# A masked graph aggregation on one core: x loaded from two queues, layernorm's scale moved behind the matmuls, differences in batches of four

## The reference, cut to what matters

```python
h = jnp.maximum(_layernorm(x, axis=-1), 0.0)        # x: 4096 x 64
support = h @ weight                                # 64 x 64
mask = (adj != 0)                                   # adj: 4096 x 4096, ones at random, 1 in 256
rank = jnp.cumsum(mask, axis=1)
deg = rank[:, -1:]
k = jnp.minimum(deg, 100.0)
pos = rank - (deg - k)
w = mask * jnp.where(pos > 0, 0.5 ** (k - pos), 0.0)
out = x + w @ support + bias
```

## Time and profile before

| | us |
|---|---|
| median of 3 runs | 232.07 (232.03 to 232.62) |
| the profiled execution | 232.5 |
| its span, first to last instruction | 230.1 |
| PE busy | 201.8 (88% of the span) |
| DVE busy | 197.7 (86%) |
| ACT busy | 163.7 (71%) |
| POOL busy | 26.0 (11%) |

### The profile page before, as it was taken

The page is one execution under the profiler, slowest core; times in us unless marked ns, Lnnn a source line. Parts: engine busy times, 40 slices in busy tenths (PEclk is TensorE's granted clock), DMA queues, the critical chain, the costliest instruction groups (busy, mean ns, idle before and its releaser), DMA issues.

```text
span 230.1 us, 6364 instructions
## 1 busy us (share of the span) xinstructions
PE 201.8 (88%) x2768; PEld 196.3 (85%) x2768; DVE 197.7 (86%) x227; ACT 163.7 (71%) x303; POOL 26.0 (11%) x53
## 2 busy tenths in 40 slices
PE   0005898899999999999999999999999899899994
PEld 0004885899999999999999999999999789899993
DVE  1799999997799989999979999969999999677053
ACT  2203489767877988878887878887889798787610
POOL 8921000411000010110010001000000000000000
PEclk9999999999999999999999999999999999999999
DMA  5999999999999999999999999999700000000001
GB/s 182 227 214 194 215 216 216 216 216 216 212 215 216 215 214 211 215 219 216 215 215 219 218 214 220 212 218 218 158 20 3 11 3 14 0 14 3 11 14 29
DMA packets 8074, 36.11 MB, mean 157 GB/s; under 512 B 1648, under 2 KB 3440, under 8 KB 3952
## 3 DMA queue, kind: packets, MB, share of 16 engines
q0 software_dynamic: 4608, 33.56, 70.1%
q1 hardware_dynamic: 3136, 2.10, 3.5%
q10 hardware_dynamic: 304, 0.07, 0.1%
HBM read 68.22 MB, written 1.05 MB: 301 GB/s over the span
## 4 chain that ended last, share of the span: by engine, by line
PE 71%; DVE 17%; issue 4%; DMA 4%; ACT 3%; POOL 1%; POOLq 0%
PE acc L570 31%; PE chain L563 22%; PE chain L561 13%; DVE masks L310 6%; DMA adj_b<-in_adj 4%; DVE part L316 3%; DVE powers L369 2%; PE acc L524 2%; ACT support L255 2%; DVE powers L362 2%; PE chain L549 1%; PE acc L514 1%; ACT powers L266 1%; DVE later L353 1%; DVE sums L344 1%
## 5 line engine op out<-in xcount | busy, mean ns | idle before, releaser
L266 ACT ACTIVATE powers<-chain 128x512 int16<-128x512 f32 (+1 forms) x282 | 152.3, 568 | 39.3 <-PE chain L563 31.3
L570 PE MATMUL acc<-support,powers 128*128 128x192 bf16 x1024 | 167.5, 246 | 2.8 <-issue 1.3
L563 PE MATMUL chain<-diag_own,masks 128*128 128x128 bf16 x640 | 125.6, 231 | 0.0
L561 PE MATMUL chain<-diag_past,masks 128*128 128x128 bf16 x596 | 118.5, 224 | 3.0 <-ACT powers L266 2.9
L570 PEld LDWEIGHTS acc<-support,powers 128*128 128x128 bf16 x1024 | 101.1, 102 | 4.5 <-DVE powers L369 1.7
L563 PEld LDWEIGHTS chain<-diag_own,masks 128*128 128x128 fp8e3 x640 | 91.0, 147 | 0.0
L561 PEld LDWEIGHTS chain<-diag_past,masks 128*128 128x128 fp8e3 x596 | 84.8, 145 | 5.0 <-ACT powers L266 4.7
L310 DVE TENSOR_SCALAR masks<-adj_b 128x4096 uint8<-128x4096 bf16 x32 | 72.9, 2279 | 3.8 <-DMA adj_b<-in_adj 3.8
L563 PE MATMUL chain<-diag_step,masks 128*128 128x128 bf16 x384 | 62.2, 220 | 0.0
L563 PEld LDWEIGHTS chain<-diag_step,masks 128*128 128x128 fp8e3 x384 | 52.1, 145 | 0.0
L206 POOL DMA_DIRECT2D adj_b<-in_adj x32 | 18.7, 585 | 116.3 <-DVE masks L310 111.8
(11 more groups left out here) (45 smaller groups left out, 53.0 us busy)
## 6 DMA issues: line engine op xcount, KB each, us to landing
adj_b<-in_adj POOLq DMA_DIRECT2D x32, 1024.0 KB, 30.3
x_sb<-in_x SPq DMA_DIRECT2D x2, 512.0 KB, 4.7
out<-x_sb SPq DMA_DIRECT2D x14, 64.0 KB, 2.6
out<-x_sb SPq DMA_DIRECT2D x4, 32.0 KB, 9.3
w<-in_L_gnn_weight ACTq DMA_DIRECT2D x2, 16.0 KB, 4.6
bias_b<-in_L_gnn_bias ACTq DMA_DIRECT2D x1, 32.0 KB, 4.5
```

Source lines behind the costliest of these rows:

```text
L266: nc.scalar.activation(powers[:, c, b, cols].bitcast(i16), chain[c][:, cols], ACT.Relu, bias=(MAX_NEIGH + 1) * STEP).then_inc(powers_ready ...
L561: nc.tensor.matmul(chain[c][:, at:at + P], column(n, t + 1), diag_past[:, :], start=False, stop=False, skip_group_check=True)
L563: return nc.tensor.matmul(chain[c][:, at:at + P], column(n, t), diag_own[:, :] if marked else diag_step[:, :], start=False, stop=True, ski ...
L570: return nc.tensor.matmul(acc[u % ACCS][:, k * 3 * D:(k + 1) * 3 * D], powers[:, u % FLIGHT, s + 1 if k < MARKS[u] else s, at:at + P], sup ...
```

## The change

- x's second half is issued by ACT's queue, ahead of the weights and the bias, instead of by SP behind the first. A half now consists of the upper or lower four rows of each eight, so that each partition's half is four pieces of 1 KB (before: two of 2 KB).
- POOL issues the first four loads of adj ahead of the six `affine_select` that build the constants. It no longer centers half 1; DVE does.
- The squares, the centered rows and the transposed rows live in the buffer `powers`; `adj_b` has 8 slots and the ring of masks 12. Unit 1's and unit 2's first `weigh` waits until these are free.
- `normalize` is gone. PE transposes the centered rows (relu commutes with a positive scale) before slot 0, and DVE multiplies the product with the weights by the reciprocal deviation where it lies, in PSUM (`scale`, four of 128 x 512). The transposes and the four products with the weights stand ahead of slot 0 (the fourth in slot 1), the parts in slots 0 to 7. The four blocks have a bank each, those of `acc`.
- Products of unit 0 start in slot 7 (before: 14); units 1 and 2 start in slots 5 and 6 (before: 5 and 10), unit 3 in slot 14 (before: 15).
- BATCH is 4. MARKS go from 2, 1, 2, 1, 1, ... to 2, 2, 0, 2, 2, 0, ... for units of two: 19 loads are marked instead of 20. Scans and halvings of a unit stand one slot earlier.
- On DVE's opening, `mask(1)` stands ahead of `scan(0, 0)`. The bias is added in four pieces, in slots 14, 17, 48 and 71.
- A way to let ACT make masks is added (`signs`), but the set of loads that would use it, `SIGNED`, is empty.

```diff
-    BATCH = 8
-    LOADS = 7
-    RING = 10
+    BATCH = 4
+    LOADS = 8
+    RING = 12
-    MARKS = [1, 1, 1, 2, 1, 2, 1, 1, 2, 1, 1, 2, 1, 1, 0, 0, 1, 1]
-    STARTS = [0, 5, 10, 15, 22, 28, 33, 39, 45, 50, 56, 62, 67, 73, 79, 84, 90, 96]
-    LAGS = [14, 10, 8, 11, 11, 11, 11, 11, 11, 11, 11, 11, 11, 11, 11, 11, 11, 8]
+    MARKS = [1, 1, 1, 2, 2, 0, 2, 2, 0, 2, 2, 0, 2, 2, 0, 0, 0, 0]
+    STARTS = [0, 5, 6, 14, 23, 27, 34, 40, 46, 51, 57, 63, 68, 74, 80, 85, 91, 97]
+    LAGS = [7, 5, 8, 11, 11, 10, 11, 10, 10, 11, 11, 12, 12, 12, 11, 11, 10, 9]
+    SIGNED = {}
...
-            return tensor[:, :, :].rearrange("p (h e t) d -> p e h t d", h=2, e=2)[:, 1 - f]
+            return tensor[:, :, :].rearrange("p (r e t) d -> p e r t d", r=RUNS, e=2)[:, 1 - f]
...
         def _(sp):
-            for f in range(2):
-                sp.dma_start(half_of(x_sb, f), half_of(x.rearrange("(p t) d -> p t d", t=T), f))\
-                  .then_inc(x_loaded[f], 16)
+            sp.dma_start(half_of(x_sb, 0), half_of(x.rearrange("(p t) d -> p t d", t=T), 0)).then_inc(x_loaded[0], 16)
...
+            for n in range(4):
+                load(n)
             pool.wait_ge(zeroed, 6)
...
-            for n in range(4):
-                load(n)
...
-            pool.wait_ge(mean_ready, 2)
-            nc.gpsimd.tensor_tensor(half_of(cen, 1), half_of(x_sb, 1), spread(mean, 1),
-                                    ALU.subtract).then_inc(cen_ready[1], 1)
...
         def _(act):
+            act.dma_start(half_of(x_sb, 1), half_of(x.rearrange("(p t) d -> p t d", t=T), 1)).then_inc(x_loaded[1], 16)
             act.wait_ge(w2_zeroed, 2)
...
+                if g == 0:
+                    part(1, 0)
+                if g == 1:
+                    part(0, 0)
+                if g == 2:
+                    part(2, 0)
+                    part(3, 0)
+                if g == 3:
+                    part(0, 1)
+                    part(1, 1)
+                if g == 4:
+                    part(2, 1)
+                    part(3, 1)
+                if g == 5:
+                    part(0, 2)
+                    part(2, 2)
+                if g == 6:
+                    part(3, 2)
+                if g == 7:
+                    part(1, 2)
...
+            def scale(i):
+
                 dve.wait_ge(ln_step, 6)
-                dve.wait_ge(cen_ready[f], 1)
-                nc.vector.tensor_tensor(half_of(cen, f), half_of(cen, f), spread(rstd, f),
-                                        ALU.mult).then_inc(unit_rows, 1)
+                dve.wait_ge(support_ready, i + 1)
+                of_block = rstd[:, :].rearrange("p (r i two) -> p r i two", i=4, two=2)[:, :, 3 - i, :]
+                block_of = split[i][:, :].rearrange("p (r two d) -> p r two d", two=2, d=D)
+                nc.vector.tensor_tensor(block_of, block_of, of_block.unsqueeze(3).to_broadcast([P, RUNS, 2, D]),
+                                        ALU.mult).then_inc(scaled[i], 1)
...
             row_sums(0)
+            means(0)
             row_sums(1)
-            means(0)
+            center(0)
             means(1)
-            center(0)
-            square_sums(0)
+            center(1)
+            sq_sums(0)
             mask(0)
+            sq_sums(1)
             halve_1(0)
-            square_sums(1)
+            variance()
+            halve_3(0)
             halve_2(0)
-            halve_3(0)
+            mask(1)
             scan(0, 0)
-            variance()
-            mask(1)
             halve_1(1)
             deviation()
             halve_2(1)
+            scale(1)
             halve_3(1)
+            scale(0)
             scan(1, 0)
-            normalize(0)
+            scale(2)
+            scale(3)
             mask(2)
...
             pe.wait_ge(consts_ready, 6)
+            turn_h(0)
+            turn_h(1)
+            make_support(0)
+            turn_h(2)
+            make_support(1)
+            turn_h(3)
+            make_support(2)
             for g in range(SLOTS):
```

More of the change, by code:

```diff
@@ L104, in gnn_decay_kernel @@
         x_sb = sb("x_sb", [P, T, D], fp32)
-        cen = sb("cen", [P, T, D], fp32)
-        h_t = sb("h_t", [P, T // 2, P], fp32)
-        sq = adj_b[:, LOADS - 1, :].bitcast(fp32).rearrange("p (t d) -> p t d", d=D)
+        own_room = powers[:, 2, :, :].rearrange("p s c -> p (s c)")
+        cen = own_room[:, 0:2 * T * D].bitcast(fp32).rearrange("p (t d) -> p t d", d=D)
+        h_t = own_room[:, 2 * T * D:4 * T * D].bitcast(fp32).rearrange("p (a b) -> p a b", b=P)
+        sq = powers[:, 1, :, :].rearrange("p s c -> p (s c)")[:, 0:2 * T * D].bitcast(fp32)\
+            .rearrange("p (t d) -> p t d", d=D)
         row_sum, mean, sq_sum, var_eps, std, rough, newton_a, newton_b, newton_c, rstd = (
@@ L122, in gnn_decay_kernel @@
         acc = [pb(f"acc{a}", [P, 512], fp32) for a in range(ACCS)]
-        turned = (acc[0], acc[1])
-        split = (acc[2], acc[3])
+        spare = pb("spare", [P, 512], fp32)
+        turned = (spare, chain[2])
+        split = acc
         x_loaded = [sem(f"x_loaded{f}") for f in range(2)]
@@ L140, in gnn_decay_kernel @@
         std_ready = sem("std_ready")
-        unit_rows = sem("unit_rows")
         h_turned = sem("h_turned")
         h_t_ready = sem("h_t_ready")
[L144 to L147, removed]
+        support_ready = sem("support_ready")
+        scaled = [sem(f"scaled{i}") for i in range(4)]
+        part_taken = [sem(f"part_taken{i}") for i in range(4)]
+        part_ready = [sem(f"part_ready{i}") for i in range(4)]
         xb_ready = sem("xb_ready")
+        signs_ready = sem("signs_ready")
         mask_ready = sem("mask_ready")
@@ L246, in turn_h, with part, signs @@
                 act.wait_ge(h_turned, i + 1)
-                t = 4 * BLOCKS[i]
-                nc.scalar.activation(h_t[:, t:t + 4, :], turned[i % 2][:, :].rearrange("p (a b) -> p a b", a=4),
+                nc.scalar.activation(h_t[:, 4 * i:4 * i + 4, :], turned[i % 2][:, :].rearrange("p (a b) -> p a b", a=4),
                                      ACT.Relu).then_inc(h_t_ready, 1)
[L251 to L256, removed]
+            def part(i, s):
+                if s:
+                    act.wait_ge(part_taken[i], s)
+                else:
+                    act.wait_ge(scaled[i], 1)
+                nc.scalar.activation(steps_of(support[:, :, s, :], i),
+                                     split[i][:, :].rearrange("p (r two d) -> p r two d", two=2, d=D),
+                                     ACT.Copy).then_inc(part_ready[i], 1)
+            def signs(n, j):
+                act.wait_ge(adj_loaded[n % LOADS], 16 * (n // LOADS + 1))
+                if n >= RING:
+                    u = UNIT_OF[n - RING]
+                    act.wait_ge(chain_ready[u % FLIGHT], taken_until(u) + TAKEN[u])
+                at = slice(j * N // PIECES, (j + 1) * N // PIECES)
+                nc.scalar.activation(masks[:, (n + SHIFT) % RING, at].bitcast(i8), adj_b[:, n % LOADS, at],
+                                     ACT.Sign).then_inc(signs_ready, 1)
             def weigh(u, b):
@@ L264, in weigh @@
                 act.wait_ge(chain_ready[c], taken_until(u) + b + 1 - (MARKS[u] == SIZES[u]))
+                if u in (1, 2) and b <= 1:
+                    if u == 1:
+                        act.wait_ge(sq_sum_ready, 2)
+                    else:
+                        act.wait_ge(support_ready, 4)
                 cols = slice(0, SIZES[u] * CHAINS[u] * P) if b else plain(u)
@@ L300, in _ @@
                             weigh(u, g - STARTS[u])
+                for n in SIGNED:
+                    if 0 <= g - SIGNED[n] < PIECES:
+                        signs(n, g - SIGNED[n])
+                if g == 0:
[18 more added lines that the diff above has]
+                    part(1, 2)
         @block.vector
@@ L305, in mask @@
             def mask(n):
+                if n in SIGNED:
+                    dve.wait_ge(signs_ready, PIECES * (1 + sum(m < n for m in SIGNED)))
+                    two = masks[:, (n + SHIFT) % RING, :].bitcast(u16)
+                    nc.vector.tensor_scalar(two, two, 0x0101, None, ALU.bitwise_and).then_inc(mask_ready, 1)
+                    return
                 dve.wait_ge(adj_loaded[n % LOADS], 16 * (n // LOADS + 1))
@@ L475, in _ @@
                         floor(u, (g - STARTS[u] - 1) // BATCH - 1)
+                if g == 14:
+                    add_bias(0)
+                if g == 17:
+                    add_bias(1)
+                if g == 48:
+                    add_bias(2)
+                if g == 71:
+                    add_bias(3)
                 for u in range(NU):
@@ L482, in _ @@
                         mask(FIRST[u] + 1)
+                    if u >= 3 and to == 7:
+                        halve_1(u)
                     if u >= 3 and to == 6:
-                        halve_1(u)
-                    if u >= 3 and to == 5:
                         halve_2(u)
@@ L490, in _ @@
```

(22 more changed lines are left out.)

103 lines of the change are left out of this document (27 added, 76 removed).

## The result

| | before | after |
|---|---|---|
| median of 4 runs, us | 232.34 (232.03 to 232.64) | 224.09 (223.27 to 224.81) |
| profiled execution | 232.5 | 224.8 |
| its span | 230.1 | 222.5 |
| PE, DVE, ACT busy | 201.8, 197.7, 163.7 | 202.5, 203.0, 161.7 |

The ratio is 0.964 (95% interval 0.960 to 0.968): 8.3 us faster, where 5.8 were forecast. (With a fourth run the kernel before has its median at 232.34, 0.3 above the one that the forecast started from.) The time lies in the range given and in the forecast's own.

The account below looks back on a forecast made before the run. PE was taken as the bound, DVE second: unit 3's base 42.6, matmuls 173.2, stalls 5.2, tail 3.3 and 2.4 outside the span make 226.7, less 0.4: 226.3 us. Range 223.5 to 235; the forecast's own 223.5 to 229.5.

Parts of the forecast that it names:

- unit 3's base: Landmark ending the opening, from which PE hardly rests: forecast at 42.6 us, against 43.02 before.
- matmuls left, at 0.082 and 0.060: PE's work after the landmark: 988 products at 0.082 us, 1536 counts and bases at 0.060, together 173.2 us.
- stalls and last drain: PE's waits after the landmark plus the final drain: 5.2 us, against 5.8 before; bounds 3 and 8.
- tail to the span's end: From PE's last product to the end of the profiled span: 3.3 us, as before.
- outside the span: Time of the profiled execution not covered by its span: 2.4 us.
- median below it: The profiled execution lay 0.4 us above the median, so 0.4 is taken off.
- ACT's pace to slot 9: In the opening, ACT's powers and parts set the pace for 12.5 us, until 36.5.
- rival 1: DVE keeps all its idle time and reaches mask 31 only at 183 us: 229.5 us in all; chance 0.16.
- rival 2: In the opening, x takes turns with adj's loads and lands after 14 us, not 6.6: 235 us; chance 0.20.

Follow-up runs that it names:

- after_again: The changed kernel run once more, unaltered (also called the repeat): 224.26 us, ratio 0.965.
- scan_first: Changed kernel with scan(0, 0) put ahead of mask(1) again: 223.72 us, ratio 0.963.
- adj_after_consts: Changed kernel with adj's first four loads issued behind the six constants again: 224.57 us, ratio 0.967.
- opening_alone: Changed kernel's opening and starts with the MARKS of before, BATCH 8 and lags of 11 from unit 3 to 16: 233.74 us, ratio 1.006.
- tables alone: Kernel before with only BATCH 4 and the changed kernel's MARKS, its own starts, lags and opening: 227.31 us, ratio 0.979.
- x_one_queue: Changed kernel with x's second half issued on SP's queue behind the first half: 240.35 us, ratio 1.033.
- x_one_adj_late: Changed kernel with both halves of x on SP's queue and adj's first loads behind the constants: 224.78 us, ratio 0.968.
- both_fillers: Changed kernel with scan(0, 0) ahead of mask(1) and 44 filler matmuls behind the fourth product with the weights: 223.31 us, ratio 0.961.
- pe_kept_busy: Changed kernel with 44 filler matmuls into an idle PSUM bank where PE idles before slot 2: 223.55 us, ratio 0.962.
- no_bias: Changed kernel without the four bias additions and their waits, so the output lacks the bias: 223.74 us, ratio 0.962.
- batch_8: Changed kernel with differences over eight steps (BATCH 8 for 4), its marks, starts and lags kept: 247.11 us, ratio 1.059.

## Why the prediction was right, and where it was off

| term | predicted | measured |
|---|---|---|
| unit 3's base | 42.6 | 42.02 (40.99 in the repeat) |
| matmuls left, at 0.082 and 0.060 | 173.2 | 173.2 |
| stalls and last drain | 5.2 | 219.23 - 42.02 - 173.2 = 4.0 |
| tail to the span's end | 3.3 | 3.3 |
| outside the span | 2.4 | 2.3 |
| profiled execution | 226.7 | 224.8 |
| median below it | 0.4 | 0.7 |

**The landmark** was near, though one step in it was wrong. It came 0.6 us early in the first profile and 1.6 in the second, where the low clock lasted half as long, so on the second it is the larger miss; I had 41.5 for a clock that stays up. adj's first load was to land 1.7 us earlier. It was issued 1.8 us earlier and mask(0) still started at 11.90, where it was 11.8 before: adj's packets came behind x's. The cost was small, since DVE was not at mask(0) before 11.15 in any case. Unit 0's base (20.45 for 19.9), its first power (23.6 for 23.4) and `scale` (0.689 for 0.65) came as worked out, and so did ACT's pace to slot 9 (37.1 for 36.5). That PE had to wait 2.1 us for the weights was not foreseen; it cost nothing that scan_first or adj_after_consts could find.

**The matmuls** were a count from the program, and the numbers left at unit 3's base are those of the trace, 988 and 1536. (The 36 products done by then are 28 of unit 0 and eight of unit 1, not 32 and four.) Moving products into light slots is worth its 2.6 us only because PE is the bound after them.

**The stalls** were mis-sized too, by 1.2 us. I took 2.0 us off for differences that are ready earlier. From the starts in the trace, less matmuls at the two prices, PE's stalls from slot 80 on were 2.9 us before and none after; from slot 14 to 40 they rose from 2.6 to 4.1, where I had 0.8 and 0.6 more. The third row of before that I had read, DVE's differences holding PE's weight loads for 1.7 us, showed only part of the late stalls: the rest stood there as "issue".

**DVE** did run behind PE and was no bound. Its last mask came at 181.17, inside the 176 to 183 worked out, its busy time rose by 5.3 us (6.6 predicted), the differences took 31.6 us for 26. Taking 2.7 us off it gained nothing that can be told from zero. What rival 1 feared, a start made earlier that DVE gives back, does happen without the slack: opening_alone, the same opening with the tables of before, loses 1.5 us. The three numbers don't add: tables alone 5.0 us faster, opening alone 1.5 us slower, both 8.3 us faster. Of the 8.3, some 4.7 are there only with both. My sum had them as terms side by side, and a reader who took the opening's terms alone from it would have forecast a gain. The sum came out because all its terms were changed at once.

**x** was there at 6.0, so rival 2 did not come true, but its mechanism is real and the margin small: the second half issued 0.7 us later, in its first half's queue, turns 224 into 240. I had priced it at 235 and put its edge at a landing of 12.4 us. x_one_queue landed at 25.3 and lost 16.3 us, so a microsecond of landing cost 0.84 us. The Trainium skill says that a DMA engine goes round its queues packet by packet (DMA: Bandwidth & Descriptors, "Queues, rings and completion order"). The stragglers of x_one_queue agree with it; the pieces of x that were ahead of adj did not take turns with anything, and the second half's first pieces came only behind the first half's, although in another queue. The same page ("Issuing engines are not separate DMA queues") says that issuing from several engines saves only the sequencer's time. For x's speed that holds (x_one_adj_late is as fast). But beside adj's early loads the second queue, with its issue 0.69 us earlier, was worth 16 us, and I had put it at nothing. Whether those 0.69 us did it, as the page would have it, or the queue as such, no run shows.

**What the falls of the clock cost.** In the profiles, a low clock for 3.4 us costs nothing at unit 3's base: it comes at 40.9 to 41.0 in after_again, scan_first and both_fillers, and at 40.9 to 41.3 in the four variants without a fall. Longer falls go with a later base, 42.02 in the changed kernel (6.8 us) and 41.60 in adj_after_consts (10.2 us). Of the eight runs of the changed kernel the two with a clock of 1.0 throughout took 223.3 and 223.8 us, the one with the long fall 224.8, the five others 223.7 to 224.5. So the falls can explain about a microsecond between runs of one kernel, more than pe_kept_busy, scan_first or no_bias differ from it.

**What stays open.** Why the clock falls in one execution and not in the next; whether x's second half was saved by its own queue or by its earlier issue; and what in opening_alone and in batch_8 costs how much.

## What to carry to other kernels

When two engines are both full, as PE and DVE are here, moving one ahead pays only if the other's results are due with slack; look at how many slots lie between an instruction and its first reader, not only at its busy time, and measure schedule and start together, since either alone can mislead. A small load that everything waits for had better be with the DMA engines before a large stream is: issuing half of x 0.7 us earlier, from a second engine, was worth 16 us here.

## What the runs showed of the hardware

- As far as the packets' times tell, the two queues of x did not share a DMA engine, although both halves were issued at 0.74 us: the first half's closing packets start from 3.57 us on and the second half's pieces from 3.57 on; the second half's closing packets start from 4.93 on, and so do adj's packets.
- In the changed kernel, what came to an engine after adj's loads took longer, by turns with them as it seems: the weights, 32 KB in all, landed 9.7 us after issue where they had taken 4.6, the bias 15.1 against 4.5. In x_one_queue the turns can be read: a late piece of x, one of adj's packets of 0.63 us, the next piece.
- The granted clock fell to 0.5 from 25.3 to 32.2 us, after PE had idled for 3 of the 5 us from 19 to 24. In other runs of the same kernel it fell for half that time, in two of eight not at all, and not in the profiles of pe_kept_busy and no_bias. In batch_8 it fell in the middle of the kernel, behind stalls of 3.3, 4.5 and 3.8 us; behind one of 3.3 us at 21 us and one of 2.9 at 234 it did not.
- The mean that is printed leaves out the time before the clock's first rise. In the kernel before that rise is at 29.2 us, so its early counts, 0.10 apart, ran at the low level of 1.2 GHz although 1.00 is printed. In the changed kernel, which has transposes and products on PE from 8.8 us, it is at 18.5: a group of products with the weights took 1.92 us at 15.60 and 1.22 at 18.16.
